# The first attention of a fused transformer kernel: scores once, held in SBUF between a running maximum and the exponential

## Chip, core and metric

The kernel runs on one core of one Trainium2 chip. The metric is the device time of one execution in microseconds (us). The engines are TensorE (PE; PEld is its weight load), VectorE (DVE), ScalarE (ACT), GpSimd (POOL) and SyncE (SP), which here only issues DMAs. Each works through its own queue in order and waits on semaphores that the others raise.

## The reference

The program is six sublayers on x of 2,048 tokens by 256 features. The change touches the second, a causal attention with latent keys and 16 heads:

```python
q = (_rmsnorm(x @ w_q_a, q_a_ln) @ w_q_b).reshape(b, s, H, DQ)      # H = 16, DQ = 128 + 64
ckv = x @ w_kv_a                                                    # 64 latents, 64 rotated
kv = (_rmsnorm(c_kv, kv_a_ln) @ w_kv_b).reshape(b, s, H, DN + DV)
...
scores = jnp.einsum('bqhd,bkhd->bhqk', qf, kf) * scale
scores = jnp.where(mask[None, None], scores, jnp.finfo(scores.dtype).min)
p = jax.nn.softmax(scores, axis=-1)
o = jnp.einsum('bhqk,bkhd->bqhd', p, v).reshape(b, s, H * DV)
return o @ w_out
```

## The kernel before

All six stages run one behind the other in `macaron_program`. The stage in question is `latent_heads`, inside `latent_attention_stage`. The weights of keys and values are folded into the queries and the output, so that all heads share one set of keys of 128 numbers a token (`key_hi`, `key_lo`: a number split into two parts of lower precision) and one set of values, `latent`, of 64.

Heads are taken in 8 pairs (`PAIRS`). For each pair the queries are taken in 4 chunks j of 512 columns (`CH`), and for chunk j the keys in 4(j+1) tiles of 128 (`key_tiles`); the last four tiles of a chunk are on the diagonal and are 512, 384, 256 and 128 queries wide. A pair has 40 key tiles for each of its two heads.

Scores stand with keys on partitions and queries in the free dimension, which suits the value matmul but not a maximum over keys. So the kernel computes scores twice:

- Maxima (`maxima`, L1020 and L1023 with the mask): one matmul of less precision with queries on partitions, for each head, tile of queries i and chunk of keys; VectorE reduces each from PSUM (L1231). Per head `shift` makes a row maximum (L1238) and a diagonal matrix of its negative (L1241), which TensorE spreads over all partitions (`spread`, L1028), and ScalarE copies to `lath_shift` (L1099).
- Scores (`scores`, L995, L996, L999, mask L998): three matmuls into one of three PSUM banks. VectorE adds the shift while reading the bank and writes `lath_shifted` (L1224). ScalarE takes the exponential into `lath_probs` (L1113). Two tiles later TensorE multiplies by the values (`values`, L1007), head 0 into the lower and head 1 into the upper 64 partitions of one bank, and GpSimd adds the tile to a running sum `lath_summed` (L1190).

At the end of a chunk, `sums`, `turn_sums`, `spread_inverse` and `project` (L1067, L1074, L1081, L1088) divide by the sum and project to x (L1264, L1270). Ahead of a chunk, `query` (L1037) makes the folded queries, and they are rotated: a cosine product, the sum and the low part on GpSimd (L1197, L1201, L1206), two sine products of 32 partitions on VectorE (L1248, L1249), the high part on ScalarE (L1138). Per pair of heads there are weights to turn and fold; `fold_out` (L1059) is one of these and runs once a pair.

The order is written out by hand: tables such as `LATENT_MAXIMA_STEPS` place each event at a fraction of a key tile, and all engines walk the same list. Pairs 1 to 6 are a loop with registers.

Of the kernel before, what the change touches and what calls it, by code (L numbers as in the profile page):

```python
# [6 lines left out]
F32 = mybir.dt.float32  # L7
# [30 lines left out]
KT_PER_PAIR = sum(TPC * (j + 1) for j in range(NCH))  # L38
# [707 lines left out]
FIRST_QUERY_STEPS = [(-21.0, -20.6), (-17.0, -15.9), (-6.0, -5.6), (8.5, 10.5)]  # L750
SUMS_STEPS = (0.5, 1.0, 1.5, 2.35, 3.5)
FIRST_HEAD_SHARE = (0.5, 0.5, 0.5, 0.5)
SPREAD_AFTER = [(0.5, 0.5), (0.25, 0.25), (0.3, 0.3), (0.5, 0.5)]
WEIGHT_STEPS = (-25.9, -25.3, -23.0, 5.85)
QUERY_AFTER = (0.3, 0.9, 1.7)
LATENT_LAG = 2
PROB_SLOTS = 5


def latent_preparation(query_steps=LATENT_QUERY_STEPS):  # L760

    out = []  # L770

    def on_tensor(step, kind, j, *rest, after=0.5):
        out.extend([(step, j, (kind, j, *rest)), (step + after, j, (kind + "_out", j, *rest))])

    on_tensor(WEIGHT_STEPS[0], "turn_q_weights", 0)
    on_tensor(WEIGHT_STEPS[1], "turn_kv_weights", 0)
    on_tensor(WEIGHT_STEPS[2], "fold_query", 0)
    out += [(WEIGHT_STEPS[2] + 0.7, 0, ("split_weights", 0)), (WEIGHT_STEPS[2] + 1.2, 0, ("split_weights_low", 0))]
    on_tensor(WEIGHT_STEPS[3], "fold_out", 0)
    for j in range(NCH):  # L780
        for h in range(2):
            at = query_steps[j][h]
            on_tensor(at, "query", j, h, after=QUERY_AFTER[0])
            out += [(at + QUERY_AFTER[1], j, ("rotate", j, h)), (at + QUERY_AFTER[2], j, ("split", j, h))]
        start, end = LATENT_MAXIMA_STEPS[j]
        main = [[("maxima", j, h, i, kc) for i in range(TPC) for kc in range(j + 1)] for h in range(2)]
        middle = start + FIRST_HEAD_SHARE[j] * (end - start)
        for h, (begun, done) in enumerate(((start, middle), (middle, end))):
            out += [(begun + n * (done - begun) / len(main[h]), j, event) for n, event in enumerate(main[h])]
            out.append((done - 0.01, j, ("shift", j, h)))  # L790
            on_tensor(done + SPREAD_AFTER[j][h], "spread", j, h, after=0.3)
        done = (STEPS_BEFORE[j] + key_tiles(j)) % KT_PER_PAIR + LATENT_LAG
        m = j if j < NCH - 1 else -1
        on_tensor(done + SUMS_STEPS[0], "sums", m, after=0.3)
        on_tensor(done + SUMS_STEPS[1], "turn_sums", m, after=0.3)
        on_tensor(done + SUMS_STEPS[2], "spread_inverse", m, after=0.3)
        for n in range(2):
            on_tensor(done + SUMS_STEPS[3 + n], "project", m, n, after=0.3)
    return sorted(out, key=lambda e: e[0])


def latent_schedule(first, last):

    placed = []
    for step, _, event in latent_preparation():
        j = event[1]
        if step >= 0 and not (first and j < 0):  # L810
            placed.append((step, event))
        elif step < 0 and not last:
            placed.append((step + KT_PER_PAIR, in_chunk(event, j, j + NCH)))
    placed.sort(key=lambda e: e[0])
    events = []
    for j in range(NCH):
        for kt in range(key_tiles(j)):
            lag = LATENT_LAG
            follow = (j, kt - lag) if kt >= lag else (j - 1, key_tiles((j - 1) % NCH) - lag + kt)
            atoms = [[("scores", j, kt, 0)], [("scores", j, kt, 1)], []]  # L820
            if not (first and j == 0 and kt < lag):
                atoms[2] += [("values", *follow, h) for h in range(2)]
                if kt == lag - 1:
                    atoms[2].append(("drain", j - 1))
            for n, atom in enumerate(atoms):
                events += atom
                while placed and placed[0][0] < STEPS_BEFORE[j] + kt + (n + 1) / len(atoms):
                    events.append(placed.pop(0)[1])
    return events + [event for _, event in placed]


LATENT_PROLOGUE = [event for step, _, event in latent_preparation(FIRST_QUERY_STEPS) if step < 0]
LATENT_EPILOGUE = ([("values", -1, key_tiles(NCH - 1) - LATENT_LAG + i, h) for i in range(LATENT_LAG) for h in range(2)] + [("drain", -1)]
                   + [(kind + out, -1) for kind in ("sums", "turn_sums", "spread_inverse") for out in ("", "_out")]
                   + [("project" + out, -1, n) for n in range(2) for out in ("", "_out")])
ON_SIDE = ("turn_q_weights", "turn_kv_weights", "fold_query", "fold_out", "query", "spread")
LATENT_SIDE_PER_PAIR = sum(event[0] in ON_SIDE for _, _, event in latent_preparation())
LATENT_SIDE_BEFORE = sum(event[0] in ON_SIDE for event in LATENT_PROLOGUE)


def with_latent_uses(events, start, earlier=()):

    out, uses = [], dict(earlier)
    for e in events:
        if e[0] in ON_SIDE:
            uses[e] = start
            e, start = (*e, start), start + 1
        elif e[0][-4:] == "_out" and e[0][:-4] in ON_SIDE:
            e = (*e, uses[(e[0][:-4], *e[1:])])
        elif e[0] == "split_weights":  # L850
            e = (*e, uses["fold_query", e[1]])
        elif e[0] == "rotate":
            e = (*e, uses["query", e[1], e[2]])
        elif e[0] == "scores":
            e = (*e, uses["spread", e[1], e[3]])
        out.append(e)
    return out, {in_chunk(e, e[1], e[1] - NCH): use - LATENT_SIDE_PER_PAIR for e, use in uses.items()}


def latent_heads(core, qa_t, key_hi, key_lo, latent, rope, raw):  # L860
# [5 lines left out]
    QW, KVW = 2 * DQ, 2 * (DN + DV)  # L866
    with ExitStack() as ctx:
        def sb(name, shape, dt=F32):
# [6 lines left out]


# [3 lines left out]
        turn_a, turn_b = sb("turn_a", [P, 2, CH]), sb("turn_b", [P, 2, CH])  # L880
        query = sb("query", [P, 2, CH])
        query_hi, query_lo = sb("query_hi", [P, NCH, 2, CH], F32R), sb("query_lo", [P, NCH, 2, CH], F32R)
        maxima = sb("maxima", [P, 2, TPC, NCH])
        row_max = sb("row_max", [P, 2, TPC])
        shift_diag = sb("shift_diag", [P, 2, TPC, P], F32R)
        shift = sb("shift", [P, 2, 2, CH])
# [4 lines left out]
        out_whole, out_t, sums_t = sb("out_whole", [P, CH]), sb("out_t", [P, CH]), sb("sums_t", [P, CH])  # L891
        inverse = sb("inverse", [P, TPC, 2])
        wide = sums_t[:].rearrange("p (t h c) -> p t h c", t=TPC, h=2)
        score_bank = [ctx.enter_context(nc.psum_tensor(f"lath_score{i}", [P, CH], F32)) for i in range(3)]
        max_bank = [ctx.enter_context(nc.psum_tensor(f"lath_max{i}", [P, CH], F32)) for i in range(2)]
        out_bank = ctx.enter_context(nc.psum_tensor("lath_out", [P, CH], F32))
        end_bank = ctx.enter_context(nc.psum_tensor("lath_end", [P, CH], F32))
        side_bank = ctx.enter_context(nc.psum_tensor("lath_side", [P, CH], F32))
        names = ("q_kv_loaded out_loaded vector_constants"
                 " scores_done shift_added exp_done values_done"  # L900
                 " maxima_done maxima_taken row_max_done diag_ready side_done side_free"
                 " cosine_done sine_done query_whole query_hi_done query_lo_done"
                 " rotation_weights_ready query_weights_ready weights_high_done weights_split"
# [9 lines left out]

        def pairs(engine, run):

            run(prologue, 0)
            run(first, 0)
            with engine.Fori(1, PAIRS - 1) as pair:
                run(middle, pair)
# [1037 lines left out]
```

## Time and profile before

| | |
|---|---|
| time, median of 3 | 2211.37 us (2203.29 to 2222.01) |
| the profiled execution's own time | 2215.39 us |
| its span, first to last instruction | 2213.7 us |
| TensorE busy | 1940.7 us, 88% |
| VectorE busy | 1626.8 us, 73% |
| ScalarE busy | 921.0 us, 42% |
| GpSimd busy | 991.4 us, 45% |
| mean granted clock of TensorE | 0.918 of 2.4 GHz |

The page also divides the span into 40 slices of 55 us. Each digit is the busy share of an engine in tenths, and PEclk the granted clock:

```profile
PE   4756999999999999999999999977497899999996
PEld 3634555555555555555555555536364344444436
DVE  6766877877877877868868778747766887788726
ACT  1132444443343443343443443431123366777771
POOL 0014687586695685695695695630231100000010
PEclk8766999999999999999999999987697788999998
```

The attention that changes is the long even part, slices 3 to 27. "Busy" of TensorE counts from a matmul's start to its modelled end, and matmuls overlap, so that times of neighbouring matmuls must not be added up. A mean in ns is the time of one instruction; a wait for another engine's memory access lies inside an instruction's time, and a wait on a semaphore lies outside.

### The profile page before, as it was taken

Reading aid. Unit: us, or ns where it says so; the run is one execution under the profiler, and the core shown is the slowest. Engines: PE = TensorE matmul, PEld = TensorE weight load, DVE = VectorE, ACT = ScalarE, POOL = GpSimd, SP = SyncE. Lnnn points to the kernel's source line nnn. Section 1 sums busy time; section 2 is a strip of 40 time slices with the busy share of each in tenths; the row PEclk is TensorE's granted clock in tenths of the full one; section 3 lists DMA queues with packets and bytes.
Section 4 is the critical chain, followed back from the end, with each engine's and each line's share of the span. In section 5 each row is a group of like instructions: output and inputs, shape, how many; then the busy total and the mean of one; then the engine's idle time right before and its main releaser. Section 6 shows DMA issues by size and latency. Waiting matters only on the chain. (4 is left out here: it accounts for less than half of the span.)

```text
span 2213.7 us, 33049 instructions
## 1 busy us (share of the span) xinstructions
PE 1940.7 (88%) x10136; PEld 1107.0 (50%) x10136; DVE 1626.8 (73%) x2798; ACT 921.0 (42%) x1883; POOL 991.4 (45%) x892
## 2 busy tenths in 40 slices
PE   4756999999999999999999999977497899999996
PEld 3634555555555555555555555536364344444436
DVE  6766877877877877868868778747766887788726
ACT  1132444443343443343443443431123366777771
POOL 0014687586695685695695695630231100000010
PEclk8766999999999999999999999987697788999998
DMA  2200000000000000000000000010233020020001
GB/s 88 69 8 0 6 8 6 9 1 6 8 0 6 8 0 6 8 1 5 8 1 5 0 1 1 1 41 1 74 67 68 1 30 1 1 30 2 2 1 38
DMA packets 26709, 34.26 MB, mean 15 GB/s; under 512 B 5312, under 2 KB 19648, under 8 KB 26432
## 3 DMA queue, kind: packets, MB, share of 16 engines
q1 hardware_dynamic: 25360, 31.28, 5.9%
q10 hardware_dynamic: 1200, 1.31, 0.2%
q8 instruction: 54, 0.88, 0.2%
q14 instruction: 95, 0.78, 0.1%
HBM read 26.03 MB, written 6.29 MB: 15 GB/s over the span
## 5 line engine op out<-in xcount | busy, mean ns | idle before, releaser
L1113 ACT ACTIVATE lath_probs<-lath_shifted 128x512 f32<-128x512 f32 (+3 forms) x640 | 358.0, 565 | 685.6 <-DVE lath_shifted L1224 647.4
L1190 POOL TENSOR_TENSOR lath_summed<-lath_summed,lath_probs 128x512 f32<-128x512 f32 (+3 forms) x528 | 585.0, 1130 | 123.1 <-ACT lath_probs L1113 113.2
L1224 DVE TENSOR_TENSOR lath_shifted<-lath_score,lath_shift 128x512 f32<-128x512 f32 (+3 forms) x640 | 385.6, 607 | 149.2 <-PE lath_score L999 134.1
L1231 DVE TENSOR_REDUCE lath_maxima<-lath_max 128x1 f32<-128x512 f32 (+3 forms) x640 | 380.3, 605 | 132.8 <-PE lath_max L1020 85.8
L1878 ACT ACTIVATE atth_probs<-atth_score 128x512 f32<-128x512 f32 (+3 forms) x640 | 293.3, 541 | 165.8 <-PE atth_score L1797 163.6
L1837 DVE TENSOR_REDUCE atth_maxima<-atth_slot 128x2 f32<-128x1024 f32 (+3 forms) x288 | 286.2, 1042 | 61.4 <-PE atth_slot L1780 60.0
L1007 PE MATMUL lath_out<-lath_probs,lat_latent 128*64 128x512 f32 (+3 forms) x1280 | 308.9, 562 | 0.0
L1020 PE MATMUL lath_max<-lat_key_hi,lath_query_hi 128*128 128x512 f32 (+3 forms) x640 | 266.0, 424 | 17.4 <-DVE lath_maxima L1231 15.8
L995 PE MATMUL lath_score<-lath_query_hi,lat_key_hi 128*128 128x512 f32 (+3 forms) x640 | 266.7, 417 | 3.9 <-DVE lath_shifted L1224 3.9
L999 PE MATMUL lath_score<-lath_query_hi,lat_key_lo 128*128 128x512 f32 (+3 forms) x640 | 256.4, 401 | 0.0
L1725 POOL TENSOR_SCALAR_AFFINE_SELECT atth_probs<-atth_probs 128x512 f32<-128x512 f32 x64 | 40.8, 637 | 443.1 <-ACT atth_probs L1878 443.1
L996 PE MATMUL lath_score<-lath_query_lo,lat_key_hi 128*128 128x512 f32 (+3 forms) x640 | 237.6, 371 | 0.0
L1197 POOL TENSOR_TENSOR lath_turn_a<-lath_query,lat_rope 128x512 f32<-128x512 f32 x64 | 93.6, 1463 | 268.1 <-ACT lath_query L1099 268.1
L1020 PEld LDWEIGHTS lath_max<-lat_key_hi,lath_query_hi 128*128 128x128 f32 x640 | 123.6, 196 | 158.1 <-DVE lath_maxima L1231 84.3
L995 PEld LDWEIGHTS lath_score<-lath_query_hi,lat_key_hi 128*128 128x128 f32 x640 | 125.5, 196 | 117.2 <-issue 57.2
L1810 PE MATMUL atth_out<-atth_probs,att_v_one 128*32 128x512 f32 (+3 forms) x1280 | 158.5, 570 | 0.6 <-POOL atth_probs L1725 0.5
L999 PEld LDWEIGHTS lath_score<-lath_query_hi,lat_key_lo 128*128 128x128 f32 x640 | 126.7, 198 | 17.3
L996 PEld LDWEIGHTS lath_score<-lath_query_lo,lat_key_hi 128*128 128x128 f32 x640 | 124.5, 195 | 12.7
L1797 PE MATMUL atth_score<-atth_query,att_key 50*128 50x512 f32 (+3 forms) x384 | 121.6, 475 | 2.0 <-ACT atth_probs L1878 1.3
L1201 POOL TENSOR_TENSOR lath_query<-lath_turn_a,lath_turn_b 128x512 f32<-128x512 f32 x64 | 81.9, 1280 | 78.2 <-DVE lath_turn_b L1249 75.9
L1007 PEld LDWEIGHTS lath_out<-lath_probs,lat_latent 128*64 128x64 f32 x1280 | 66.4, 136 | 91.6 <-issue 65.3
L1797 PEld LDWEIGHTS atth_score<-atth_query,att_key 50*128 50x128 f32 x384 | 54.1, 197 | 96.1 <-ACT atth_probs L1878 79.1
(342 smaller groups left out, 2794.9 us busy)
## 6 DMA issues: line engine op xcount, KB each, us to landing
att_first_query<-att_scratch SPq DMA_DIRECT2D x12, 256.0 KB, 8.9
atth_query<-att_scratch SPq DMA_DIRECT2D x12, 256.0 KB, 9.0
ffn_a_w<-in_L_ffn_W SPq DMA_DIRECT2D x2, 1024.0 KB
lat_raw_out<-in_L_attn_w_out SPq DMA_DIRECT2D x8, 256.0 KB, 2.7
lat_rope<-in_c_rope_feature SPq DMA_DIRECT2D x1, 2048.0 KB, 10.5
ffn_b_w<-in_L_ffn_W SPq DMA_DIRECT2D x2, 1024.0 KB, 7.1
mix_a_factors<-in_L_ffn_factors SPq DMA_DIRECT2D x8, 256.0 KB, 4.2
att_scratch<-attp_high SPq DMA_DIRECT2D x4, 512.0 KB, 3.3
```

The source lines that it names most:

```text
L995: nc.tensor.matmul(out, key_hi[:, keys], hi, start=True, stop=False)
L996: nc.tensor.matmul(out, key_hi[:, keys], lo, start=False, stop=False)
L999: nc.tensor.matmul(out, key_lo[:, keys], hi, start=False, stop=True).then_inc(s["scores_done"], 1)
L1007: mm = nc.tensor.matmul(out_bank[64 * h:64 * h + 64, q0:CH], latent[:, kt, 0:KL], probs[:, prob_slot(j, kt), h, q0:CH], start=(kt == 0), s ...
L1020: mm = nc.tensor.matmul(bank[:, 0:width], query_hi[:, nj, h, i * P:(i + 1) * P], key_hi[:, kc * CH:kc * CH + width], start=True, stop=(kc ...
L1113: nc.scalar.activation(probs[:, prob_slot(j, kt), h, q0:CH], shifted[:, 2 * (kt % 2) + h, q0:CH], ACT.Exp, scale=SCALE0).then_inc(s["exp_d ...
L1190: last = nc.gpsimd.tensor_tensor(summed[:, j % 2, h, q0:CH], so_far, probs[:, prob_slot(j, kt), h, q0:CH], ALU.add)
L1224: nc.vector.tensor_tensor(shifted[:, 2 * (kt % 2) + h, q0:CH], score_bank[score_place(j, kt, h) % 3][:, q0:CH], shift[:, j % 2, h, q0:CH], ...
L1231: nc.vector.reduce_max(maxima[:, h, i, kc:kc + 1], max_bank[(i * (nj + 1) + kc) % 2][:, 0:width], AX.X).then_inc(s["maxima_taken"], 1)
L1797: nc.tensor.matmul(score_bank[u % 3][:, q0:CH], key_rows(GROUP * g + h, PLACED + 2, kt * P, P), query_rows(n, h, PLACED + 2, q0, CH - q0), ...
L1837: nc.vector.reduce_max(maxima[:, n % 2, :, pair, i, at], slot[r % 2][:, :, begin:begin + width], AX.X)\
L1878: nc.scalar.activation(probs[:, step % PROB_STEPS, h, q0:CH], score_bank[u % 3][:, q0:CH], ACT.Exp, scale=SCALE1)\
```

## The change

The work is divided anew, into units of one head of one chunk (64 `LATENT_UNITS`), and steps of two key tiles of one head (320 `LATENT_STEPS`).

- The maxima matmuls, their masks and their reductions go.
- `scores`: the same three matmuls a tile, for two key tiles, into a PSUM tile of two banks (two of these).
- `evac` (ScalarE, L1077 of the new kernel): copies the raw scores from PSUM to one of 14 slots of `lath_held` in SBUF.
- `max` (VectorE, L1192): running elementwise maximum of the held scores over the key tiles, in `lath_largest`, 128x1024 elements for a whole step and 128 to 512 for the tiles on the diagonal. At the unit's end both halves are joined, TensorE transposes (`turn_max`), VectorE reduces and forms the diagonal, then `spread` as before.
- `add` (VectorE, L1239): adds the shift to the held scores in place. `exp` (ScalarE, L1082): exponential in place.
- `values`: two key tiles of one head stand side by side in the two halves of a bank; at the unit's end ScalarE copies one half (`drain`) and VectorE adds the other (`fold`, L1265).
- `sum` (GpSimd, L1169 and L1160): as before, tile by tile, from the held slots. The rotation is as before (L1175, L1179, L1184 on GpSimd; L1248, L1249 on VectorE).
- `sums` puts the sums on partitions directly (L1011), and `turn_sums` goes.
- `latent_plan` computes the order of each engine with durations for each event, a second pass 12 steps behind the first (`SECOND_PASS_AFTER`); all 8 pairs are written out without a loop.

The core of the diff:

```diff
-LATENT_MAXIMA_STEPS = [(-12.0, -2.0), (0.2, 3.15), (3.5, 11.25), (12.2, 22.7)]
...
+HELD_STEPS = 14
+SECOND_PASS_AFTER = 12.0
+QUERY_SLOTS = 3
...
+        add("tensor", 0.1 + 3 * total / 2250, g, ("scores", g), ("low", u), of("scores", g - 1), of("evac", g - 2))
+        add("scalar", on_scalar, g, ("evac", g), ("scores", g), of("values", held), of("sum", held))
...
+        add("vector", elementwise, late - 1.0, ("add", g), ("spread_out", u), ("max", g), of("add", g - 1))
+        add("scalar", on_scalar, late - 0.6, ("exp", g), ("add", g), of("exp", g - 1))
...
-        shifted = sb("shifted", [P, 4, CH])
-        probs = sb("probs", [P, PROB_SLOTS, 2, CH])
-        summed = sb("summed", [P, 2, 2, CH])
...
+        largest = sb("largest", [P, 2, 2, CH])
...
+        held = sb("held", [P, HELD_STEPS, 2, CH])
+        summed = sb("summed", [P, 2, CH])
...
-                            nc.vector.tensor_tensor(shifted[:, 2 * (kt % 2) + h, q0:CH], score_bank[score_place(j, kt, h) % 3][:, q0:CH],
-                                                    shift[:, j % 2, h, q0:CH], ALU.add).then_inc(s["shift_added"], 1)
-                        elif kind == "maxima":
...
-                            nc.vector.reduce_max(maxima[:, h, i, kc:kc + 1], max_bank[(i * (nj + 1) + kc) % 2][:, 0:width],
-                                                 AX.X).then_inc(s["maxima_taken"], 1)
...
+                            nc.scalar.activation(slot(n)[:, tiles, q0:CH], score_bank[n % 2][:, tiles, q0:CH], ACT.Copy)\
+                              .then_inc(s["evacuated"], 1)
...
+                    nc.vector.tensor_tensor(out, first, second, ALU.max).then_inc(s["maxed"], 1)
...
+                            raise_largest(top, slot(n - 1), slot(n), 0)
+                        elif step:
+                            for tiles, q0 in step_parts(n):
+                                raise_largest(top[:, tiles, q0:CH], top[:, tiles, q0:CH], slot(n)[:, tiles, q0:CH], before)
...
+                            nc.vector.tensor_tensor(slot(n)[:, tiles, q0:CH], slot(n)[:, tiles, q0:CH],
+                                                    shift[:, u % 2, q0:CH].unsqueeze(1).broadcast_to([P, count, CH - q0]), ALU.add)\
+                              .then_inc(s["shift_added"], 1)
```

VectorE's queue before, in a chunk of four key chunks: `lath_score` and `lath_max` are PSUM banks.

```order
L1224 TENSOR_TENSOR lath_shifted<-lath_score,lath_shift 128x512
...
L1231 TENSOR_REDUCE lath_maxima<-lath_max 128x1
...
L1224 TENSOR_TENSOR lath_shifted<-lath_score,lath_shift 128x512
...
L1231 TENSOR_REDUCE lath_maxima<-lath_max 128x1
...
L1231 TENSOR_REDUCE lath_maxima<-lath_max 128x1
```

VectorE's queue now, in a unit of the widest chunk: `lath_held`, `lath_largest`, `lath_shift` and `lath_query` are in SBUF, `lath_out` is in PSUM.

```order
L1239 TENSOR_TENSOR lath_held<-lath_held,lath_shift 128x1024
L1192 TENSOR_TENSOR lath_largest<-lath_largest,lath_held 128x1024
L1239 TENSOR_TENSOR lath_held<-lath_held,lath_shift 128x1024 x2
L1192 TENSOR_TENSOR lath_largest<-lath_largest,lath_held 128x1024
L1239 TENSOR_TENSOR lath_held<-lath_held,lath_shift 128x1024
L1265 TENSOR_TENSOR lath_out_whole<-lath_out,lath_half 64x512
L1192 TENSOR_TENSOR lath_largest<-lath_largest,lath_held 128x1024
L1239 TENSOR_TENSOR lath_held<-lath_held,lath_shift 128x512
L1239 TENSOR_TENSOR lath_held<-lath_held,lath_shift 128x384
L1192 TENSOR_TENSOR lath_largest<-lath_largest,lath_held 128x512
L1192 TENSOR_TENSOR lath_largest<-lath_largest,lath_held 128x384
```

Instructions that read PSUM have given way to ones that read two operands from SBUF; adds of an earlier unit alternate with maxima of a later one.

GpSimd's queue now, in the same part of a pair: sums of exponentials, and the three instructions of the rotation between them.

```order
L1169 TENSOR_TENSOR lath_summed<-lath_summed,lath_held 128x512 x2
L1175 TENSOR_TENSOR lath_turn_a<-lath_query,lat_rope 128x512
L1169 TENSOR_TENSOR lath_summed<-lath_summed,lath_held 128x512 x2
L1179 TENSOR_TENSOR lath_query<-lath_turn_a,lath_turn_b 128x512
L1169 TENSOR_TENSOR lath_summed<-lath_summed,lath_held 128x512 x2
L1184 TENSOR_TENSOR lath_query_lo<-lath_query,lath_query_hi 128x512
```

The whole stage has the same number and widths of these as before (592 sums, 192 of the rotation); they only stand in another order.

## Rows read from the trace of the kernel before

**Rows 1.** Windows of the stage and of two pairs; columns stand in the first line.

```profile
core 0: us, PE busy (x) PEld busy (x) DVE busy (x) ACT busy (x) POOL busy (x), PEclk, DMA share, GB/s
143.00:1471.00 1328.00, 1218.77 (x5536) 696.40 (x5536) 998.66 (x1686) 534.20 (x1025) 911.08 (x784) 0.96 0.01 4
...
220.70:381.00 160.30, 149.94 (x698) 85.34 (x698) 125.14 (x212) 67.30 (x130) 114.82 (x99) 0.99 0.02 5
541.30:701.60 160.30, 150.35 (x694) 86.00 (x693) 123.55 (x211) 66.34 (x128) 113.90 (x99) 0.98 0.02 5
```

**Rows 2.** Two lines of the kernel: number, ns least/median/most, first and last start.

```profile
L1059 PE MATMUL lath_side<-lat_raw_out,lath_kv_w_t x32: 379/404/430, 220.7 to 1342.6; 128*64 128x256 f32 x32
...
L1224 DVE TENSOR_TENSOR lath_shifted<-lath_score,lath_shift x640: 233/682/694, 193.7 to 1457.9; 128x512 f32<-128x512 f32 x128, 128x256 f32<-128x256 f32 x32
```

**Rows 3.** TensorE's longest wait over seven pairs.

```profile
engine line waited for: us in total, times, longest us
PE lath_side L1028 <- DVE lath_shift_diag L1241: 32.5, 28, 1.6
```

**Rows 4.** GpSimd and VectorE in order of time, GpSimd idle.

```profile
start us, us, engine line op out<-in xcount [idle before <-releaser]
398.90 0.69 DVE L1248 TENSOR_TENSOR lath_turn_b<-lath_query,lat_rope 32x512 f32<-32x512 f32 x1
...
400.38 1.28 POOL L1201 TENSOR_TENSOR lath_query<-lath_turn_a,lath_turn_b 128x512 f32<-128x512 f32 x1 [3.60 <-DVE lath_turn_b L1249]
```

**Rows 5.** The same two engines where GpSimd works, 347.7 to 352.4 us.

```profile
347.69 1.29 POOL L1190 TENSOR_TENSOR lath_summed<-lath_summed,lath_probs 128x512 f32<-128x512 f32 x1
...
349.12 1.54 POOL L1190 TENSOR_TENSOR lath_summed<-lath_summed,lath_probs 128x512 f32<-128x512 f32 x1
...
349.56 1.65 DVE L1249 TENSOR_TENSOR lath_turn_b<-lath_query,lat_rope 32x512 f32<-32x512 f32 x1
...
350.62 1.73 POOL L1190 TENSOR_TENSOR lath_summed<-lath_summed,lath_probs 128x512 f32<-128x512 f32 x1
```

**Rows 6.** Groups of instructions by line and shape, 190 to 1470 us.

```profile
line engine op names shapes xcount | busy us, mean ns | idle before us <-releasers
...
L1224 DVE TENSOR_TENSOR lath_shifted<-lath_score,lath_shift 128x512 f32<-128x512 f32 x448 | 307.1, 688 | 123.8 <-PE lath_score L999 112.1 <-ACT lath_shift L1099 3.0 <-issue 1.4
...
L1113 ACT ACTIVATE lath_probs<-lath_shifted 128x512 f32<-128x512 f32 x448 | 279.4, 630 | 427.2 <-DVE lath_shifted L1224 395.4 <-POOL lath_summed L1190 26.4
...
L1241 DVE TENSOR_TENSOR lath_shift_diag<-lath_minus_ident,lath_row_max 128x512 fp32r<-128x512 f32 x63 | 63.1, 1001 | 2.2
L1249 DVE TENSOR_TENSOR lath_turn_b<-lath_query,lat_rope 32x512 f32<-32x512 f32 x58 | 62.2, 1072 | 1.8
...
L1248 DVE TENSOR_TENSOR lath_turn_b<-lath_query,lat_rope 32x512 f32<-32x512 f32 x58 | 59.3, 1022 | 1.8
...
L1099 ACT ACTIVATE lath_shift<-lath_side 128x512 f32<-128x512 f32 x63 | 36.7, 583 | 14.5 <-PE lath_side L1028 14.4
L1224 DVE TENSOR_TENSOR lath_shifted<-lath_score,lath_shift 128x384 f32<-128x384 f32 x64 | 35.5, 554 | 7.8 <-PE lath_score L999 5.7 <-ACT lath_probs L1113 0.6
...
L1113 ACT ACTIVATE lath_probs<-lath_shifted 128x384 f32<-128x384 f32 x64 | 33.5, 524 | 53.7 <-DVE lath_shifted L1224 47.6 <-PE lath_out L1007 4.1 <-POOL lath_summed L1190 1.4
```

**Rows 7.** The page's rows of three lines, all shapes together.

```profile
L1224 DVE TENSOR_TENSOR lath_shifted<-lath_score,lath_shift 128x512 f32<-128x512 f32 (+3 forms) x640 | 385.6, 607 | 149.2 <-PE lath_score L999 134.1
L1231 DVE TENSOR_REDUCE lath_maxima<-lath_max 128x1 f32<-128x512 f32 (+3 forms) x640 | 380.3, 605 | 132.8 <-PE lath_max L1020 85.8
...
L1020 PE MATMUL lath_max<-lat_key_hi,lath_query_hi 128*128 128x512 f32 (+3 forms) x640 | 266.0, 424 | 17.4 <-DVE lath_maxima L1231 15.8
```

**Rows 8.** Windows around changes of TensorE's clock, columns as in Rows 1.

```profile
366.00:516.00 150.00, 140.12 (x656) 80.07 (x654) 115.41 (x194) 62.23 (x120) 104.49 (x89) 1.00 0.02 6
...
1465.10:1485.60 20.50, 8.50 (x29) 6.70 (x30) 14.80 (x58) 2.69 (x4) 0.00 (x0) 0.50 0.38 109
1485.60:1499.20 13.60, 10.88 (x61) 6.43 (x59) 5.08 (x11) 5.43 (x8) 0.00 (x0) 1.00 0.00 1
```

More of the change, by code:

```diff
@@ L753 @@
[L753 to L799, printed above, removed]
@@ L802, in latent_schedule @@
[L802 to L829, printed above, removed]
@@ L832 @@
[L832 to L857, printed above, removed]
+LATENT_UNITS = [(pair, j, h) for pair in range(PAIRS) for j in range(NCH) for h in range(2)]
@@ new lines, in max_parts, with sum_parts, running @@
+def max_parts(g):
+    u, s = LATENT_STEPS[g]
+    j = LATENT_UNITS[u][1]
+    if j and s == 0:
+        return 0
+    return len(step_parts(g)) + (1 if j and s == 2 * j + 1 else 0)
+def sum_parts(g):
+    u, s = LATENT_STEPS[g]
+    return 1 if s == 0 and LATENT_UNITS[u][1] else 2
+def running(counts):
+    total, out = 0, []
+    for n in counts:
+        total += n
+        out.append(total)
+    return out
+PARTS_DONE = running(len(step_parts(g)) for g in range(len(LATENT_STEPS)))
+MAX_DONE = running(max_parts(g) for g in range(len(LATENT_STEPS)))
@@ L879, in latent_heads @@
         w_value = sb("w_value", [P, DIM])
-        turn_a, turn_b = sb("turn_a", [P, 2, CH]), sb("turn_b", [P, 2, CH])
+        turn_a, turn_b = sb("turn_a", [P, CH]), sb("turn_b", [P, CH])
         query = sb("query", [P, 2, CH])
[L882 to L886, printed above, removed]
@@ new lines, in latent_heads @@
+        largest = sb("largest", [P, 2, 2, CH])
+        row_max = sb("row_max", [P, TPC])
+        shift_diag = sb("shift_diag", [P, TPC, P], F32R)
+        shift = sb("shift", [P, 2, CH])
+        held = sb("held", [P, HELD_STEPS, 2, CH])
+        summed = sb("summed", [P, 2, CH])
+        half, out_whole, out_t = sb("half", [P, CH]), sb("out_whole", [P, CH]), sb("out_t", [P, CH])
+        inverse, wide = sb("inverse", [P, TPC, 2]), sb("wide", [P, TPC, 2, KL])
+        score_bank = [ctx.enter_context(nc.psum_tensor(f"lath_score{i}", [P, 2, CH], F32)) for i in range(2)]
@@ L914, in pairs @@
[L914 to L919, printed above, removed]
-            run(final, PAIRS - 1)
-            run(LATENT_EPILOGUE, PAIRS)
-        def chunk(pair, j):
-            return pair * NCH + j
-        def step_unit(pair, j, kt):
-            return pair * KT_PER_PAIR + KT_PER_PAIR * (j // NCH) + STEPS_BEFORE[j % NCH] + kt
-        def score_unit(pair, j, kt, h):
-            return step_unit(pair, j, kt) * 2 + h
@@ L951, in maxima_unit, with side, freed @@
[L951 to L960 removed]
+        side_free = [core.sem(f"lath_side_free{i}") for i in range(2)]
+        def side(event):
+            return side_bank[use[event] % 2]
+        def freed(event):
+            return side_free[use[event] % 2]
@@ L962, in latent_heads, with wait_side, slot @@
+        def wait_side(engine, event):
+            engine.wait_ge(s["side_done"], use[event] + 1)
+        def slot(g):
+            return held[:, g % HELD_STEPS]
         with nc.Block() as block:
```

742 lines of the change are left out of this document (420 added, 322 removed).

## Prediction, made before the changed kernel ran

> **What bounds the kernel now.** I read the windows first, to find where the stage lies and which engine fills it. The stage that changes takes 1,328 of the 2,213.7 us [rows 1]. In two stretches of one pair's length TensorE is busy 150 of 160.3 us, VectorE 124 to 125, GpSimd 114 to 115 and ScalarE 66 to 67 [rows 1]. The length of a pair is a difference of starts: L1059 (`fold_out`, four records a pair) runs first at 220.7 and last at 1342.6 us, seven pairs apart, so (1342.6 - 220.7) / 7 = 160.3 us [rows 2]. Eight pairs are 1,282 us; 46 us are left for filling and draining the stage. Then I read TensorE's waits, since it is the fullest. Its longest, for `lath_shift_diag`, is 32.5 us over seven pairs, under 5 a pair [rows 3]. So TensorE is the bound, with 10 us of idleness a pair, and the change takes work from it: a good place to cut. The question is who is next, and GpSimd at 114 us cannot be ignored.
>
> The last view is the one I rest most on: single instructions of VectorE and GpSimd in time. Where GpSimd is idle, `lath_turn_b` on VectorE, which has **both inputs in SBUF**, takes 0.69 us at 512 elements (at 398.90 us; GpSimd starts at 400.38, idle for 3.60 before) [rows 4]. At 349.56 us the same instruction takes 1.65 us: GpSimd is then in an instruction that began at 349.12 and took 1.54, to 350.66, and `lath_turn_b` ends at 351.21, 0.55 us after it. The GpSimd instruction behind, begun at 350.62, takes 1.73 us, where an undisturbed one took 1.29 [rows 5]. The two take turns: VectorE waits for the end of GpSimd's instruction, and GpSimd's next one is held up for 1.73 - 1.29 = 0.44 us. VectorE's means show it too: the two `lath_turn_b` instructions take 1,022 and 1,072 ns and `lath_shift_diag` 1,001 ns, while the add of L1224, as wide but with one input in PSUM, takes 688 [rows 6]. Today few VectorE instructions meet GpSimd so: two `turn_b` and one `shift_diag` per unit, 24 a pair.
>
> The Trainium skill has a rule for this (SBUF — State Buffer, section "SBUF: two separate sides"): a VectorE instruction with two SBUF inputs and a GpSimd instruction exclude each other, each for its whole length. The trace agrees that they exclude each other; by 0.44 us against 0.69 it does not agree on the whole length. Taken at its word the rule gives the second rival below.
>
> **The change, part by part.** *Removed:* 640 maxima matmuls with their masks and 640 reductions from PSUM. The matmuls are 266 us over the eight pairs [rows 7], 33 a pair, in durations that overlap with their neighbours'; with the masks 20 to 40 us leave; with the 32 small transposes a pair (`turn_max`) and the rest of the edge work, TensorE needs 110 to 130 us a pair. The value matmuls are as many and as wide; that the two halves of the bank now hold two key tiles and not two heads costs and gives nothing.
>
> *ScalarE* gets an evacuation as large as its exponential. L1113 takes 630 and 524 ns at 512 and 384 elements [rows 6], 0.83 ns an element, so 1.05 us at 1,024. A pair has 24 steps of 1,024 and 8 of each diagonal width: exponentials 24 x 1.05 + 8 x 1.9 = 40 us, evacuations by L1099's 583 ns for 512 [rows 6] some 38, and 36 side copies of about 0.6 us another 22. That is 100 us a pair, no bound.
>
> *GpSimd* does what it did: 50 adds of 512, 8 each of 384, 256 and 128, and 24 instructions of the rotation, 98 a pair. I charge today's busy time, 114.3 us a pair [rows 1].
>
> *VectorE* is where it turns. Both new kinds of work, the running maximum (L1192) and the in-place add of the shift (L1239), read two SBUF operands, where both old kinds read PSUM. Per pair: adds 24 x 1,024 and 8 each of 512, 384, 256, 128; maxima 18 x 1,024, 12 x 512, 8 each of 384, 256, 128. That is 110 instructions with 65,536 elements. The add of 512 takes 688 ns and of 384 takes 554 [rows 6]: 134 ns for 128 elements, 1.05 ns an element, and 0.15 us fixed. At 512 elements a visit between two GpSimd instructions cost GpSimd 0.44 us, which is 1.05 x 512 less 0.10: the fixed parts lie beside each other.
> - GpSimd as today: 114.3 us.
> - 110 new visits: 1.05 ns x 65,536 - 110 x 0.10 = 68.8 - 11.0 = 57.8 us.
> - The 24 old visits: many miss GpSimd today, most will not; their means (about 1.03 us against 0.69) say half do. 12 x 0.44 = 5 us.
> - 134 visits among 98 GpSimd instructions: at least 36 follow another visit directly, and save nothing (0.10) and leave a small gap (0.05, an estimate): 5 us.
> - Time in which neither has the operands: VectorE has 134 x 0.15 = 20 us of fixed parts and some 20 us from PSUM (8 reductions and 8 folds new, 8 additions to x, 4 `out_t`). GpSimd can run under those 40 us, if it has something to do. The bounds are 0 and 40. I take 10, near the low end, since today GpSimd's instructions stand back to back over long stretches and the new lookahead is long (a second pass 12 steps behind the first, 14 slots).
>
> Sum 192 us a pair against 160.3. Filling and draining: today the first add of L1224 comes at 193.7 us [rows 2], 50 us after the stage's start; the maxima of the first chunk no longer stand ahead of it, so 30 us instead of 46. The stage: 8 x 192 + 30 = 1,566 us instead of 1,328. The rest of the profiled execution is 2,215.4 - 1,328 = 887, and 887 + 1,566 = 2,453 us. The profiled execution lies 4 us over the median: **2,450 us**.
>
> *What is queued behind a held instruction.* VectorE's queue has maxima of later steps between adds of earlier ones. While it is held, `evac` gets no further than the 14 slots and TensorE no further than the two score banks, so TensorE goes idle. Loads, straight-line code instead of the loop, and the end of each chunk (`turn_sums` gone, one more fold) I cost at nothing: they lie under the 192 us; without that cover the edge work would be the 4 to 5 us of a chain `turn_max`, reduction, diagonal, spread, copy per unit, and the lookahead of six or more steps covers it. ScalarE has `evac` some 7 to 9 steps ahead of `exp`, so the reuse of a slot leaves GpSimd five steps of room.
>
> **The rivals.**
> 1. *Faster: the turns cost little*, because GpSimd and VectorE fall into gaps of one another. Then VectorE's own work decides: 68.8 + 110 x 0.15 = 85, its other work 28 (124 less the 96 that L1224 and L1231 are in [rows 7]), 11 new from PSUM: 125 us a pair, and with some jitter 128, under which ScalarE's 100, GpSimd's 114 and TensorE's 120 fit. 887 + 8 x 128 + 30 = 1,941 us. The point that decides: the kernel stays as it is at 162 us a pair, where of the 77.7 us that I add to GpSimd's 114.3 only 47.7 are paid, 61%. Against it: VectorE's visits and GpSimd's work are together longer than the pair, so there are no gaps to fall into, and [rows 5] is plain. Chance 0.06.
> 2. *Each visit costs GpSimd its whole length.* 85.3 instead of 57.8 us: 114.3 + 5 + 85.3 + 10 = 215 a pair, 887 + 8 x 215 + 30 = 2,637 us. [Rows 5] speaks against it at 512 elements; at 1,024 nothing in this trace shows it. Chance 0.08.
> 3. *TensorE's clock becomes the bound.* At 110 to 130 us of work in 192 it would idle a third of the time. From 1,465.1 us, with 8.5 of 20.5 us busy, the clock stands at 0.50, and in 366 to 516 us, with 140 of 150 busy, at 1.00 [rows 8]. At 1.2 GHz throughout, 120 us of work become 240: 887 + 8 x 240 + 30 = 2,837 us. Against it: at 0.50 TensorE would be full, and of the stretch from 1,485.6 us, 10.9 of 13.6 busy, the row shows 1.00 [rows 8]. It will flicker, and cost little. Chance 0.04.
>
> **How the numbers follow.** The forecast has 0.82. Its bounds: 177 a pair (nothing back to back, nothing uncovered) give 887 + 1,416 + 25 = 2,328; 222 (all 40 us uncovered) 887 + 1,776 + 35 = 2,698. Eight times in ten I expect 181 to 208 a pair, 2,370 to 2,590 us; what is left out is rival 1 below and most of rivals 2 and 3 above. Under 1% either way (about what a measurement can tell from no change) is a narrow strip, 0.02; faster 0.06; slower 0.92.
>
> **What would show it.** Right: the adds of L1239 at 1,024 elements have a mean near 2 us, where 1.05 x 1,024 + 0.15 = 1.2 us would be undisturbed; GpSimd's adds of 512 have a mean near 1.7 to 2.3 where [rows 5] has 1.29 alone; `fold_out` returns every 192 us; TensorE is busy about two thirds, with its clock between 0.7 and 0.95. Wrong: L1239 near 1.2 us at a pair of about 128 us (rival 1); GpSimd's 512 held up by over 1.2 us behind a visit of 1,024 (rival 2); TensorE over 90% busy at a clock near 0.5 (rival 3).

## The result

| | before | changed kernel |
|---|---|---|
| time, median | 2214.47 us (2203.29 to 2222.01, 4 runs) | 2528.28 us (2526.53 to 2546.02, 4 runs) |
| ratio to before | | 1.143, 95% interval 1.136 to 1.150 |
| the profiled execution's own time | 2215.39 us | 2546.02 us |
| its span | 2213.7 us | 2544.3 us |
| the stage (first to last instruction of it) | 1,328 us | 1,646 us |
| TensorE's granted clock in the stage | 0.96 | 0.84 |

The changed kernel is 14% slower: 2,528 us where 2,450 was forecast with 2,370 to 2,590 around it. The stage took 318 of the 331 us between the two profiled executions. The rest of the program took 755 us instead of 742, without a change in its code; its clock was 0.84 instead of 0.87.

The windows of the stage and of what follows it, after the change (the columns are those of [rows 1], busy us and number of instructions of each engine):

```profile
core 0: us, PE busy (x) PEld busy (x) DVE busy (x) ACT busy (x) POOL busy (x), PEclk, DMA share, GB/s
143.00:1789.00 1646.00, 1240.77 (x5152) 733.14 (x5152) 1490.13 (x1414) 769.51 (x1281) 1239.09 (x784) 0.84 0.01 4
1789.00:2544.00 755.00, 651.97 (x3972) 348.31 (x3972) 527.13 (x834) 354.11 (x753) 79.88 (x104) 0.84 0.13 26
```

VectorE ran fewer instructions (1,414 against the 1,686 of [rows 1]) and was busy for 1,490 us instead of 999. GpSimd ran the same 784 instructions in 1,239 us instead of 911. TensorE lost 384 matmuls and was busy for 1,241 of 1,646 us instead of 1,219 of 1,328. Over eight pairs that is 186 us of VectorE and 155 of GpSimd in 206 us.

The groups that carry it, after (line, engine, operation, names, shapes, count, busy us, mean ns, idle before, its cause):

```profile
L1169 POOL TENSOR_TENSOR lath_summed<-lath_summed,lath_held 128x512 f32<-128x512 f32 x336 | 586.8, 1746 | 34.2 <-ACT lath_held L1082 8.9
L1239 DVE TENSOR_TENSOR lath_held<-lath_held,lath_shift 128x1024 f32<-128x1024 f32 x192 | 352.5, 1854 | 9.4 <-ACT lath_shift L1088 8.5
...
L1192 DVE TENSOR_TENSOR lath_largest<-lath_largest,lath_held 128x1024 f32<-128x1024 f32 x96 | 167.6, 1746 | 1.2 <-ACT lath_held L1077 0.9
```

An add or a maximum of 1,024 elements took 1.85 and 1.75 us in the mean, where 1.2 was worked out for one that is left alone. These means are mixtures: of the 336 adds and maxima of 1,024 that touch `lath_held`, 124 took under 1.3 us and 165 over 1.9, up to 2.35. GpSimd's add of 512 took 1.75 us, where [rows 5] has 1.29 for an undisturbed one. In order of time, three instructions of the stage:

```profile
828.28 1.41 POOL L1169 TENSOR_TENSOR lath_summed<-lath_summed,lath_held 128x512 f32<-128x512 f32 x1
828.48 2.30 DVE L1239 TENSOR_TENSOR lath_held<-lath_held,lath_shift 128x1024 f32<-128x1024 f32 x1
829.77 1.86 POOL L1169 TENSOR_TENSOR lath_summed<-lath_summed,lath_held 128x384 f32<-128x384 f32 x1
```

GpSimd is in an instruction until 829.69. The add, begun at 828.48, ends at 830.78, 1.09 us after that, and GpSimd's next one, of 384 elements, takes 1.86 us. It is the picture of [rows 5], at twice the width.

### The profile page after: what moved, and what is told of

Read it like the earlier page. It is cut to its first block and busy times, and to the rows that moved or that the text cites. A ratio compares the mean times of both kernels' runs of the same rounds, so it can differ in the third digit from the quotient of the medians.

```text
span 2544.3 us, 28168 instructions
## 1 busy us (share of the span) xinstructions
PE 1976.3 (78%) x9752; PEld 1149.9 (45%) x9752; DVE 2118.9 (83%) x2526; ACT 1157.0 (45%) x2139; POOL 1319.2 (52%) x892
## 3 DMA queue, kind: packets, MB, share of 16 engines
q8 instruction: 79, 1.29, 0.2%
## 5 line engine op out<-in xcount | busy, mean ns | idle before, releaser
L1169 POOL TENSOR_TENSOR lath_summed<-lath_summed,lath_held 128x512 f32<-128x512 f32 (+3 forms) x528 | 798.5, 1512 | 53.3 <-ACT lath_held L1082 14.1
L1239 DVE TENSOR_TENSOR lath_held<-lath_held,lath_shift 128x512 f32<-128x512 f32 (+1 forms) x448 | 605.7, 1389 | 9.7 <-ACT lath_shift L1088 8.5
L1082 ACT ACTIVATE lath_held<-lath_held 128x512 f32<-128x512 f32 (+1 forms) x448 | 314.2, 720 | 479.8 <-DVE lath_held L1239 478.8
L1192 DVE TENSOR_TENSOR lath_largest<-lath_largest,lath_held 128x256 f32<-128x256 f32 (+3 forms) x336 | 398.0, 1207 | 4.0 <-ACT lath_held L1077 1.2
L996 PE MATMUL lath_out<-lath_held,lat_latent 128*64 128x512 f32 (+3 forms) x1280 | 360.8, 624 | 29.3 <-ACT lath_held L1082 29.1
L1077 ACT ACTIVATE lath_held<-lath_score 128x512 f32<-128x512 f32 (+1 forms) x448 | 291.1, 683 | 170.4 <-PE lath_score L985 149.9
L1175 POOL TENSOR_TENSOR lath_turn_a<-lath_query,lat_rope 128x512 f32<-128x512 f32 x64 | 106.2, 1659 | 265.7 <-ACT lath_query L1106 265.4
L1002 PE MATMUL lath_side<-square,lath_largest 128*128 128x128 f32 x256 | 56.3, 361 | 166.0 <-DVE lath_largest L1192 165.8
L1184 POOL TENSOR_TENSOR lath_query_lo<-lath_query,lath_query_hi 128x512 fp32r<-128x512 f32 x64 | 108.5, 1696 | 80.2 <-ACT lath_query_hi L1111 80.1
L1179 POOL TENSOR_TENSOR lath_query<-lath_turn_a,lath_turn_b 128x512 f32<-128x512 f32 x64 | 115.3, 1801 | 60.1 <-DVE lath_turn_b L1249 55.8
L1025 PE MATMUL lath_side<-lath_w_value,lath_out_t 128*128 128x256 f32 x256 | 87.4, 493 | 64.2 <-issue 56.5
L1160 POOL TENSOR_TENSOR lath_summed<-lath_held 128x512 f32<-128x512 f32 x48 | 95.4, 1988 | 77.2 <-ACT lath_held L1082 74.2
```

What stands on the lines that cost most here:

```text
L996: last = nc.tensor.matmul(out_bank[u % 2][KL * i:KL * i + KL, q0:CH], latent[:, kt, 0:KL], slot(n)[:, i, q0:CH], start=(step == 0), stop=( ...
L1077: nc.scalar.activation(slot(n)[:, tiles, q0:CH], score_bank[n % 2][:, tiles, q0:CH], ACT.Copy)\
L1082: nc.scalar.activation(slot(n)[:, tiles, q0:CH], slot(n)[:, tiles, q0:CH], ACT.Exp, scale=SCALE0)\
L1169: nc.gpsimd.tensor_tensor(total[:, q0:CH], so_far, slot(n)[:, i, q0:CH], ALU.add).then_inc(s["tiles_summed"], 1)
L1192: nc.vector.tensor_tensor(out, first, second, ALU.max).then_inc(s["maxed"], 1)
L1239: nc.vector.tensor_tensor(slot(n)[:, tiles, q0:CH], slot(n)[:, tiles, q0:CH], shift[:, u % 2, q0:CH].unsqueeze(1).broadcast_to([P, count, ...
```

## The experiments

The runs were taken in three groups, each with the kernel before beside it (medians 2206.6, 2209.0 and 2210.2 us); the ratios are to that neighbour. Differences in us to the changed kernel are of medians from different groups, so some 8 us of them are not certain.

### The price of a turn by itself

A kernel of its own with eight stretches, in which independent instructions run beside each other. Its core:

```python
@block.gpsimd
def _(pool):
    for i in range(n_pool):
        nc.gpsimd.tensor_tensor(pool_out[:, i, :], src[:, 0, 0:CH], src[:, 1, 0:CH], ALU.add)
...
@block.vector
def _(dve):
    for i in range(dve_ops):
        ...
        elif kind == "two1024":
            nc.vector.tensor_tensor(dve_out[:, i, :], src[:, 2, :], src[:, 3, :], ALU.add)
        ...
        elif kind == "one1024":
            nc.vector.tensor_tensor(dve_out[:, i, :], bank[:], src[:, 3, :], ALU.add)
```

> This kernel leaves the whole computation out (it writes zeros) and runs eight short stretches of independent instructions: twelve GpSimd adds of 512 alone; twelve VectorE adds with two SBUF inputs alone, of 512 and of 1,024; then twelve GpSimd adds beside VectorE adds with two SBUF inputs of 512, of 1,024 and of 128; then beside VectorE adds of 1,024 and of 512 with one input in PSUM. My theory (the two take turns, and a VectorE visit between two GpSimd instructions costs GpSimd 1.05 ns an element less 0.10 us): GpSimd 1.24 us an instruction alone, 1.68 beside 512, 2.2 beside 1,024, 1.27 beside 128, and 1.24 beside VectorE instructions that have an input in PSUM. By the rival (a visit costs its whole length) 1.93, 2.47 and 1.5 us. If they shared the port without turns, VectorE's own time would be stretched evenly and its duration would not depend on where GpSimd's instruction ends.

GpSimd's twelve adds of 512 in order of time (start, us in all): alone, beside VectorE's adds of 512 with two SBUF inputs, of 1,024, of 128, and beside adds of 1,024 with one input in PSUM:

```profile
19.07 14.68 POOL L1939 TENSOR_TENSOR pool_out<-src 128x512 f32<-128x512 f32 x12 [18.63 <-PEq L1935]
...
56.72 19.60 POOL L1939 TENSOR_TENSOR pool_out<-src 128x512 f32<-128x512 f32 x12 [22.98 <-ACTq L1935]
...
78.69 25.46 POOL L1939 TENSOR_TENSOR pool_out<-src 128x512 f32<-128x512 f32 x12 [2.37 <-ACTq L1935]
...
108.16 15.20 POOL L1939 TENSOR_TENSOR pool_out<-src 128x512 f32<-128x512 f32 x12 [4.01 <-ACTq L1935]
...
124.93 14.73 POOL L1939 TENSOR_TENSOR pool_out<-src 128x512 f32<-128x512 f32 x12 [1.57 <-ACTq L1935]
```

The first of the twelve is not held up, so eleven share the difference to 14.68 us: (19.60 - 14.68) / 11 = 0.45 us for a visit of 512, (25.46 - 14.68) / 11 = 0.98 for 1,024, and 0.05 for 128. The prediction's price, 1.05 ns an element less 0.10 us, gives 0.44, 0.98 and 0.03. Beside an operand in PSUM the adds take 14.73 us: no turn at all. A visit does not cost its whole length: VectorE's twelve adds of 1,024 took 13.71 us alone, 1.14 each. Nor is an add with an operand in PSUM shorter by itself: fourteen took 15.93 us beside GpSimd, again 1.14 each. VectorE's adds of 1,024, with two SBUF inputs alone and with one input in PSUM beside GpSimd:

```profile
42.40 13.71 DVE L1947 TENSOR_TENSOR dve_out<-src 128x1024 f32<-128x1024 f32 x12 [0.63 <-PEq L123]
...
124.94 15.93 DVE L1951 TENSOR_TENSOR dve_out<-bank,src 128x1024 f32<-128x1024 f32 x14 [0.63 <-PEq L123]
```

Where both inputs are in SBUF, the two instructions take turns, one by one:

```profile
86.51 2.24 POOL L1939 TENSOR_TENSOR pool_out<-src 128x512 f32<-128x512 f32 x1
...
87.55 2.28 DVE L1947 TENSOR_TENSOR dve_out<-src 128x1024 f32<-128x1024 f32 x1
...
88.71 2.24 POOL L1939 TENSOR_TENSOR pool_out<-src 128x512 f32<-128x512 f32 x1
...
89.75 2.28 DVE L1947 TENSOR_TENSOR dve_out<-src 128x1024 f32<-128x1024 f32 x1
```

So a change that gives VectorE one operand from PSUM takes its instruction out of the turns. That is what the next three runs use.

### The maximum from PSUM

```diff
+                            if MAX_DONE[n - 2]:
+                                pe.wait_ge(s["maxed"], MAX_DONE[n - 2])
...
-                                raise_largest(top[:, tiles, q0:CH], top[:, tiles, q0:CH], slot(n)[:, tiles, q0:CH], before)
+                                raise_largest(top[:, tiles, q0:CH], top[:, tiles, q0:CH], fresh[:, tiles, q0:CH], before)
```

`fresh` is `score_bank[n % 2]`; VectorE still waits for the evacuation, as in the changed kernel. The new wait is also told to the plan, which works the order of the queues out anew; so it does in the next two runs.

> As the changed kernel, but the running maximum reads the fresh scores from the PSUM bank instead of from the held copy (the first step of a unit still comes from its held copy, beside one PSUM operand), behind the evacuation; a score bank is free only when the maximum has read it too. This takes 48 of 134 visits with two SBUF inputs a pair away, 27,648 elements, and adds a wait to TensorE. Theory of turns: 27,648 x 1.05 ns - 48 x 0.10 = 24 us a pair less, so 2528 - 8 x 24 = 2335 us, between 2300 and 2400. Rival (the turns cost little, the loss is in the order of the queues and in waits): not faster, 2530 or more, since a wait is added and no instruction is shorter.

Measured: 2306.2 us median (2304.8 to 2314.4), ratio 1.048, interval 1.042 to 1.053. That is 222 us less than the changed kernel, 28 a pair where 24 were worked out. The maxima of 1,024 now take 1.21 us; the adds, which still take turns, 1.61:

```profile
L1242 DVE TENSOR_TENSOR lath_held<-lath_held,lath_shift 128x1024 f32<-128x1024 f32 x192 | 306.1, 1612 | 4.5 <-ACT lath_shift L1090 4.2
...
L1194 DVE TENSOR_TENSOR lath_largest<-lath_largest,lath_score 128x1024 f32<-128x1024 f32 x96 | 116.0, 1209 | 9.1 <-ACT lath_held L1079 7.9
```

It got faster although a wait was added, and nothing was changed in the instructions but where an operand is read. An added wait does not explain that; how much a new order could give is answered below, at "Both from PSUM" and "A plan that knows of the turns".

### The shift from PSUM

```diff
-        shift = sb("shift", [P, 2, CH])
...
-        out_bank = [ctx.enter_context(nc.psum_tensor(f"lath_out{i}", [P, CH], F32)) for i in range(2)]
+        out_bank = 2 * [ctx.enter_context(nc.psum_tensor("lath_out", [P, CH], F32))]
+        shift = ctx.enter_context(nc.psum_tensor("lath_spread", [P, CH], F32))
```

> As the changed kernel, but the spread shift stays in a PSUM bank of its own and is added from there, so that the adds have one SBUF input and one PSUM input; ScalarE's copy of it goes; for the bank, the two output banks become one, so the values of a unit wait for the fold of the unit before. This takes 56 visits a pair away, 34,816 elements. Theory of turns: 36.6 - 5.6 = 31 us a pair less, so 2528 - 248 = 2280 us, between 2240 and 2350. Rival (order and waits): 2530 or more.

Measured: 2266.5 us (2253.9 to 2270.5), ratio 1.027, interval 1.021 to 1.033; 262 us less than the changed kernel, 33 a pair where 31 were worked out. Here it is the adds that take 1.21 us and the maxima that take 1.48:

```profile
L1235 DVE TENSOR_TENSOR lath_held<-lath_held,lath_spread 128x1024 f32<-128x1024 f32 x192 | 228.5, 1209 | 23.9 <-PE lath_spread L1007 23.1
L1188 DVE TENSOR_TENSOR lath_largest<-lath_largest,lath_held 128x1024 f32<-128x1024 f32 x96 | 141.8, 1477 | 3.9 <-ACT lath_held L1078 3.5
```

### Both from PSUM

Both diffs together; nothing is left out of the computation.

> Both edits of the two runs before together: of 134 visits a pair 30 are left (rotation, diagonal, the joining of the halves), and the computation is whole. Theory of turns: the turns are off the path, and the next bound is VectorE's own work of about 125 us a pair or TensorE's 110 to 130, with the stage's new waits 130 to 145 a pair: 2528 - 8 x (205 - 138) = about 1990 us, between 1940 and 2080, and faster than the kernel before the change. Rival (order and waits): 2400 or more.

Measured: 2076.3 us (2067.6 to 2078.9), ratio **0.941**, interval 0.936 to 0.946. It is faster than both kernels: 452 us below the changed one, 6% below the one before. The saving is 56 us a pair, somewhat less than the 28 and 33 of the two edits added up, and less than the 67 that I had expected; the time is just inside the stated range. Its stage:

```profile
144.00:1333.00 1189.00, 1085.32 (x5152) 647.67 (x5152) 1061.88 (x1414) 724.76 (x1217) 967.24 (x784) 0.96 0.02 5
```

VectorE runs the same 1,414 instructions as in the changed kernel, with the same operations on the same elements, in 1,062 instead of 1,490 us, and GpSimd its same 784 in 967 instead of 1,239. What differs is the memory that an operand is read from, and what comes with it: ScalarE's 64 copies of the shift are gone, there is one output bank instead of two, and the queues have another order. Waits and order would show as idle time of VectorE, outside its instructions, and that fell by 29 us, from 156 to 127; the other 428 of the stage's 457 us are gone from inside its instructions. TensorE's clock is back at 0.96.

### GpSimd's sums made short

```diff
-                            q0 = queries_from(2 * step + i, j)
+                            q0 = CH - 16
```

> As the changed kernel, but GpSimd's 74 sums a pair add 16 columns instead of 128 to 512 (the sums of exponentials are left out but for those columns, so the division is wrong); the number of instructions, waits and slots is the same, VectorE's work is untouched. Theory of turns: GpSimd's share of the turns falls from some 108 us of work a pair to 30 for the rotation and a few for the short sums, VectorE's own work of some 125 us a pair with 30 to 40 us of remaining turns decides: 150 to 165 a pair, 2528 - 8 x (205 - 157) = about 2140 us, between 2050 and 2220. Rival (order and waits of VectorE's queue; its own instructions are the bound whatever GpSimd does): over 2400.

Measured: 2091.9 us (2090.4 to 2093.5), ratio 0.948, interval 0.943 to 0.953. With VectorE's work and every wait as in the changed kernel, but the other party of the turns cut down, 436 us go. The waits and the order of the queues cannot be the bulk of the loss. VectorE's instructions take 1,080 us of the stage instead of 1,490, without any edit to them:

```profile
141.00:1345.00 1204.00, 1092.71 (x5152) 651.65 (x5152) 1079.86 (x1415) 754.41 (x1281) 688.74 (x784) 0.96 0.02 5
```

Alone this run would leave open whether GpSimd's own speed was the bound; the run before it leaves GpSimd's work as it was and gains 452 us.

### Less work for TensorE

```diff
-                            nc.tensor.matmul(scores[:, q0:CH], key_hi[:, keys], lo, start=False, stop=False)
```

> As the changed kernel, but one of the three score matmuls is left out (the one with the low part of the queries, so the scores are less precise): some 15 us of TensorE's 110 to 130 us a pair at 2.4 GHz, 30 at 1.2 GHz. Theory of turns: TensorE is not on the path, within 1.5%: 2490 to 2540 us. Rival (TensorE at its lower clock is the bound): 8 x 15 = 120 us faster or more, 2400 or less.

Measured: 2522.7 us (2517.3 to 2528.0), ratio 1.143, interval 1.137 to 1.149: no difference. In the stage of this kernel TensorE was busy for 1,147 of 1,638 us at a mean clock of 0.79, lower still, and it cost nothing:

```profile
141.00:1779.00 1638.00, 1147.08 (x4512) 630.81 (x4512) 1484.61 (x1414) 766.68 (x1281) 1251.72 (x784) 0.79 0.01 4
```

### A plan that knows of the turns

```diff
-        elementwise = sum(0.07 + w / 960 for w in widths)
+        elementwise = sum(0.45 + w / 850 for w in widths)
...
-        add("pool", sum_parts(g) * 0.06 + (CH if sum_parts(g) == 1 else total) / 420, late, ("sum", g), ("exp", g), of("sum", g - 1),
+        add("pool", sum_parts(g) * 0.06 + (CH if sum_parts(g) == 1 else total) / 300, late, ("sum", g), ("exp", g), of("sum", g - 1),
```

> As the changed kernel, but the durations with which the order is planned are nearer to those that the trace shows: VectorE's elementwise steps 1.65 us instead of 1.14 at 1,024, GpSimd's sums 300 elements a us instead of 420, its rotation 1.75 instead of 1.3, the sine products 2.3 instead of 1.2. The same instructions stand in another order. Theory: the sum of the turns is the same, and only the idle time of both engines, some 13 to 17 us a pair, can shrink: between 2440 and 2540 us. Rival (the order is the cause of the loss): 2350 or less.

Measured: 2473.1 us (2463.4 to 2482.0), ratio 1.122, interval 1.116 to 1.128; 55 us less than the changed kernel, 7 a pair. VectorE's busy time hardly moved, from 1,490 to 1,499 us; what went is its idle time, from 156 us of the stage to 88:

```profile
141.00:1728.00 1587.00, 1231.74 (x5152) 711.39 (x5152) 1499.25 (x1414) 775.10 (x1281) 1230.23 (x784) 0.85 0.01 4
```

So a better order is worth some 55 us, a sixth of the 314 us that the changed kernel lost. The time in which GpSimd or a VectorE instruction with two SBUF inputs is running, added up from the instructions of the trace, is 1,507 us in both kernels: the new order took nothing from the turns. Where VectorE stands idle in the changed kernel its waits say (whom it waited for, us in all, times, longest):

```profile
DVE lath_turn_b L1248 <- ACT lath_query L1106: 34.8, 17, 3.4
DVE lath_inverse L1271 <- PE lath_side L1011: 25.0, 15, 8.8
DVE lath_largest L1192 <- ACT lath_held L1077: 18.2, 13, 4.2
```

The first two stand at the head of its queue for something that is late by the plan's measure, with adds and maxima behind them.

### What bounds the better kernel

Three more runs on the kernel with both operands from PSUM. Without the low part's matmul, as above:

> As the kernel with both operands from PSUM, without the low part's score matmul (scores less precise). It asks what bounds that kernel, which took 2076 us. If TensorE does (it is busy nine tenths there): 8 x 10 to 15 us less, 1960 to 2000. If VectorE does (union of its work about 133 us of 149 a pair): 2050 or more.

Measured: 2070.7 us (2070.5 to 2071.0), ratio 0.938, interval 0.934 to 0.943, against 0.941: TensorE is not its bound. With short sums:

> As the kernel with both operands from PSUM, with GpSimd's sums cut to 16 columns (sums left out but for those). If what is left of the turns (30 visits a pair) or GpSimd's 121 us of work a pair still costs that kernel something, it gets faster by the excess of those visits, 12 to 18 us a pair: 1930 to 1980 us. If VectorE's own work bounds it: 2030 or more.

Measured: 1973.4 us (1968.4 to 1978.3), ratio 0.893, interval 0.887 to 0.899; 103 us less, 13 a pair. The gain lies in the expected range. Short sums take away turns and GpSimd's own work together, but of the 97 us that the stage lost, 89 are gone from inside VectorE's instructions (973 instead of 1,062 us), which no edit touched; so the larger part is the turns of the 30 visits a pair that are left:

```profile
141.00:1233.00 1092.00, 1052.32 (x5152) 632.62 (x5152) 972.61 (x1415) 725.35 (x1217) 424.25 (x784) 0.99 0.02 5
```

With other durations in the plan:

> As the kernel with both operands from PSUM, the computation whole, with durations in the plan that fit it (VectorE's steps 1.20 us instead of 1.14 at 1,024, the sine products 2.6 instead of 1.2, GpSimd's sums 380 elements a us instead of 420, the cosine product 1.6 instead of 1.3). A better order can take part of VectorE's idle time, some 16 us a pair: 2000 to 2076 us expected; slower would say that the order was as good as these durations make it.

Measured: 2060.5 us (2047.0 to 2064.2), ratio 0.934, interval 0.929 to 0.938, against 0.941 with 0.936 to 0.946. It is the lowest of the whole kernels here, but the intervals overlap, so that this last step is not shown.

## Why the prediction was right, point by point

- **TensorE is the bound before, and it is not what decides after.** Right. 384 of its instructions went and 318 us came. Rival 3, its clock, fell with the run that left a matmul out. Its own work was put too low, at 110 to 130 us a pair: with both operands from PSUM, at the same clock of 0.96 as before the change, it was busy 1,085 / 8 = 136. That had no consequence, since TensorE was not the bound.
- **The turns.** Right in kind, and right in the price of one visit. The trace of before had 24 of these visits a pair, and one of them in detail [rows 5]; from it came 0.44 us for 512 elements, and 0.98 for 1,024 by the slope of an add. Alone they measured 0.45 and 0.98. Rival 2 (the whole length: 1.1 to 1.2 us for 1,024) fell with it, and so did rival 1: L1239 was to show 1.2 us there, and showed 1.85. The forecast was "near 2 us"; GpSimd's adds of 512 were to lie between 1.7 and 2.3, and showed 1.75. The Trainium skill (SBUF — State Buffer, section "SBUF: two separate sides") has it that whichever of the two engines starts first gets the ports that they share for the whole instruction, and that the other fully blocks. The traces agree in that each waits for the end of the other's instruction; what a visit adds to GpSimd's time is less than the visit's length alone, by 0.16 us at 1,024 elements (0.98 against 1.14).
- **GpSimd's own work, 114 us a pair, and ScalarE's 100.** GpSimd's instructions and widths were the same; with its waits for turns it was busy 155 us a pair. ScalarE was busy 769.5 / 8 = 96 us.
- **The sum of a pair.** 192 us forecast; (1,646 - 30) / 8 = 202 measured, with the forecast's own 30 us for filling and draining. The trace tells where the other 10 lie. GpSimd or a VectorE instruction with two SBUF inputs is running in 1,507 us of the stage, 188 a pair, where the forecast's first four terms come to 182. Neither is running in the other 139 us; less the 30 of filling and draining that is 14 a pair, where the forecast has 10. So both parts were put low, the turns by 6 us and the idle time by 4. Which of the terms of the turns is short is not shown. For the idle time a cause was tried. I had held the order for good enough, with a lookahead of six steps and more. But the order was planned with durations of 1.14 us for what took 1.8, and VectorE stood idle 156 / 8 = 19.5 us a pair. The run with the plan's durations put nearer left the turns at 1,507 us and took 59 us from the stage, 7 a pair, all of it time in which neither ran.
- **`fold_out` returns every 192 us.** This sign was badly chosen. The new plan does not put it at a fixed place in a pair: it first stands at 148.0 us, and the mean of seven intervals is (1630.4 - 148.0) / 7 = 212 us. The stage's length through eight, 206, is the one to read.
- **TensorE's share and clock.** "About two thirds" was 75%; the clock, expected between 0.7 and 0.95, was 0.84.
- **Outside the stage** I expected nothing. The profiled execution has 13 us more there, at a lower clock, and it is also the slowest of its four runs (2,546 against a median of 2,528); no run looked into it.

## What to carry to other kernels

Before work is moved to VectorE's SBUF-to-SBUF side, add up what VectorE does with two SBUF inputs and what GpSimd does: while both have work, their sum (less 0.16 us for each visit in the small kernel), and not the larger of the two is the floor. The price of a visit can be read from one place in a trace where a VectorE instruction with two SBUF inputs meets GpSimd. And the cure need not be less work: where one operand can stay in PSUM until VectorE has used it, here the fresh scores and the spread shift, the same VectorE and GpSimd instructions cost 56 us less of 206 a pair, and the idea that lost 14% wins 6%.

## What the runs showed of the hardware that was not expected

The turns are not always one by one. In the small kernel GpSimd's and VectorE's instructions alternated, one by one. In the changed kernel one GpSimd add of 512 elements, which takes 1.27 us at least, took 7.86:

```profile
1661.87 7.86 POOL L1160 TENSOR_TENSOR lath_summed<-lath_held 128x512 f32<-128x512 f32 x1 [2.58 <-ACT lath_held L1082]
...
1661.77 1.21 DVE L1239 TENSOR_TENSOR lath_held<-lath_held,lath_shift 128x1024 f32<-128x1024 f32 x1
1662.90 0.16 DVE L1271 RECIPROCAL lath_inverse<-lath_side 128x4 f32<-128x4 f32 x1
1663.00 1.18 DVE L1192 TENSOR_TENSOR lath_largest<-lath_largest,lath_held 128x1024 f32<-128x1024 f32 x1
1664.11 2.34 DVE L1239 TENSOR_TENSOR lath_held<-lath_held,lath_shift 128x1024 f32<-128x1024 f32 x2
1666.38 1.14 DVE L1192 TENSOR_TENSOR lath_largest<-lath_largest,lath_held 128x512 f32<-128x512 f32 x2
1667.45 1.14 DVE L1239 TENSOR_TENSOR lath_held<-lath_held,lath_shift 128x512 f32<-128x512 f32 x2
1668.62 0.69 DVE L1265 TENSOR_TENSOR lath_out_whole<-lath_out,lath_half 64x512 f32<-64x512 f32 x1
```

VectorE was at work when it began (1661.77 against 1661.87), and each of VectorE's instructions up to 1668.59 started before the one ahead of it had ended. The add came through only 1.14 us after 1668.59, beside the fold, which reads PSUM. The reciprocal at 1662.90 reads PSUM too, for 0.16 us, and the add did not get through beside it. In the small kernel VectorE's instructions also started before the end of the one ahead, and yet the two took turns; there GpSimd had begun first. Whether that decides was not tried. The case is rare: of GpSimd's 784 instructions in the stage this is the only one over 2.8 us.
